# TensorE's idle products as tiles of 64 rows by 32 columns, eight side by side, in an attention and mixture-of-experts kernel

## The chip, the cores and the metric

The kernel runs on one core of a Trainium2 chip. The metric is the device time of one execution in microseconds; the profile shows one execution of the same program.

## The reference

A sequence of T = 4096 tokens of D = 256 numbers passes through one layer: attention with 16 heads, ALiBi bias and LoRA weights, a layer norm, a mixture of 8 experts of which each token takes 2, and a second layer norm.

```python
q, k, v = (lora(x, W, A, B) for each of q, k, v)        # x @ W.T + 2 * x @ B.T @ A.T
s = q @ k.T / 4 + slope[h] * (i - j), masked to j <= i
x = layernorm(x + softmax(s) @ v @ Wp.T)
gates, experts = top2(softmax(x @ Wg))                  # capacity CAP = 1076 slots for each expert
buf[expert * CAP + place] = x                           # what exceeds CAP is dropped
y = gelu(buf @ W1 + b1) @ W2 + b2
out = layernorm(x + sum of gate * y over the two experts of a token)
```

## The kernel before, in words

The program has two parts, each with an instruction stream per engine that is written out by hand. The first part projects block by block (8 blocks of 512 tokens), attends, and routes the tokens of blocks 0 to 6 between the attention's steps. The second part (`experts`) begins with the last block's routing (`Last`), then runs over the 8 experts, and ends with the layer norm.

TensorE has *idle products* at two places. They multiply data that happen to be there, write to a PSUM bank from which nobody reads them, and stand where the engine would otherwise wait.

*Lead-in.* `pe_warm(n, bank)` (lines 658 to 660) issues n bfloat16 products of the 128 x 128 corner of `sq` (all zero here) with its 512 columns, into `ps_r`. TensorE runs 13 of them, then the LoRA products for the keys (`pe_lora`, line 654, which contract only 8 rows), 3 more, the LoRA products for the queries, and then the first tiles of the projection (`pe_tile`, line 666). VectorE adds each LoRA result to the weights (`dve_weights`, line 761), and the first tile waits for that.

*Beside the scatters.* In `Last`, TensorE counts the tokens ahead of each token (`pe_count`, lines 1866 and 1867). From the counts VectorE makes the destinations, ScalarE and VectorE split the rows into two bfloat16 parts, and GpSimd scatters them to `slots_x` in 8 indirect DMAs (line 2030), each followed by an increment of `issued`; a memset (line 2212) gives the ninth. `Last.tensor` puts idle products between its waits for `issued`: 10 ahead of the first, 3 behind each of the first seven, 9 behind the eighth, 40 in all. Each is a float32 product of 128 x 128 with 256 columns.

Behind them TensorE transposes the first expert's rows (`transpose`, line 2394), which SyncE loads into `xe` (line 2330) once all scatters are complete. ScalarE copies them to `xs` (line 2464), and the expert's first products (`up`, line 2406) need those.

Every wait is on a semaphore, and every engine works in the order of its own stream. `ps_s` is the tile of six PSUM banks that the lead-in calls `banks(0)` to `banks(5)`; in the second part `ps_y` (two banks) and `ps_x` (two banks) are others.

Of the kernel before, what the change touches and what calls it, by code (L numbers as in the profile page):

```python
# [9 lines left out]
F32 = mybir.dt.float32  # L10
# [8 lines left out]
P = 128  # L19
# [6 lines left out]
QB = 512  # L26
NB = T // QB
KT = QB // P
# [25 lines left out]
HALF = 64  # L54
# [41 lines left out]
COLS = 4  # L96
# [391 lines left out]
class Project:  # L488
# [166 lines left out]
                           start=True, stop=True)  # L655
        mm.then_inc(j.lora_mm, 1)

    def pe_warm(j, pe, n, bank):
        for _ in range(n):
            pe.matmul(bank[:], j.sq[:, 0, 0:P], j.sq[:, 0, :], start=True, stop=True)  # L660

    def pe_tile(j, pe, n, k, out):
        m = TILE_ORDER[k]
# [588 lines left out]
def attend(nc, io, sb, psum, sem, dram, attnT, sums, flag, slots_x, r, out_stored):  # L1252
    with ExitStack() as st:
# [6 lines left out]
        ps_r = psum("ps_r", [P, QB], F32, st)  # L1260
# [9 lines left out]
        j = Project(io, lambda n, sh, dt: sb(n, sh, dt, st), sem, dram, flag, o, r,  # L1270
                    Space(r.x1[:, 2:].rearrange("p n t d -> p (n t d)")), Space(words))
        last = Space(o.mem[:, (o.mem.shape[1] - QB * (NP_ - FIRST_PAIR[NB - 1])):].bitcast(F32))
# [7 lines left out]
        with nc.Block() as block:  # L1280
            @block.sync
            def _(sp):
# [13 lines left out]
                for t in range(N_TURNS):  # L1296
# [35 lines left out]
                    if t in LOAD_AT:  # L1332
                        b = LOAD_AT[t]
                        for k in range(ACCS):
                            done = [job.stores for job in JOBS if job.number % ACCS == k and any(of == b for _, of, _ in job.heads)]
                            if done:
                                sp.wait_ge(out_stored[k], max(done))
                        r.load(sp, b, 0)
# [4 lines left out]
            def _(pe):  # L1343

                pe.wait_ge(j.hsel_set, 1)
                j.pe_warm(pe, 13, ps_r)
                j.pe_lora(pe, 1, banks)
                j.pe_warm(pe, 3, ps_r)
                j.pe_lora(pe, 0, banks)
                pe.wait_ge(j.weff_done, 2)  # L1350
                j.pe_tile(pe, 0, 0, banks(0))
# [696 lines left out]
class Last:  # L2048
# [24 lines left out]
    def tensor(l, pe, out, count, warm):  # L2073
        r, u = l.r, l.N % 2
        for c in (1, 0):
            for s in range(KT):
                if c == 0 or s == 0:
                    pe.wait_ge(r.scaled, l.BASE + (KT if c == 1 else KT + s + 1))
                mm = pe.matmul(out[:, s, 0:D + E], r.aT[:, u, c, s * P:(s + 1) * P], r.wp[:, c, :], start=(c == 1), stop=(c == 0))  # L2079
                if c == 0:  # L2080
                    mm.then_inc(r.y_mm, 1)
        r.pe_count(pe, l.N, count[:, 0:KT * E])


        for m in range(2 * KT + 1):
            if m >= 1:
                pe.wait_ge(l.issued, m)
            for _ in range(10 if m == 0 else 3 if m < 2 * KT else 9):
                pe.matmul(warm[:, 0:QB // 2], r.aT[:, u, 0, 0:P], r.aT[:, u, 0, 0:QB // 2], start=True, stop=True)  # L2089

    def stats(l, dve, s):
        r = l.r
# [169 lines left out]
def experts(nc, io, psum, slots_x, result, X, r, z, last):  # L2262
    sb, sem = X.sb, X.sem
    w1s, w2s, b1, b2, ident, ws, ye_mm = X.w1s, X.w2s, X.b1, X.b2, X.ident, X.ws, X.ye_mm
    with ExitStack() as st:
        warm = sb("warm5", [1, 1], F32)
# [11 lines left out]
        ps_h = psum("ps_h", [P, 4, QB], F32, st)  # L2278
        ps_y = psum("ps_y5", [P, 2, QB], F32, st)
        ps_x = psum("ps_x", [P, 2, 2 * QB], BF16, st)  # L2280
# [44 lines left out]
        with nc.Block() as block:  # L2325
            @block.sync
            def _(sp):
                def load(u, e):
                    z = SB[0][1]
                    sp.dma_start(xe[:, u, 0:z], xs_d[e, 0:z * P].rearrange("(k p) d -> p k d", p=P)).then_inc(x_first[u], 16)  # L2330
                    sp.dma_start(xe[:, u, z:ST - 1], xs_d[e, z * P:(ST - 1) * P].rearrange("(k p) d -> p k d", p=P)).then_inc(x_loaded[u], 16)
                    sp.dma_start(xe[0:LAST, u, ST - 1], xs_d[e, (ST - 1) * P:CAP]).then_inc(x_loaded[u], 16)

                last.sync(sp, X, io)
                load(0, 0)
                load(1, 1)
                with sp.Fori(0, E // 2 - 1) as i:
                    for u in range(2):
                        e = 2 * i + u
                        sp.wait_ge(ws, e * 2 + 2)  # L2340
                        sp.wait_ge(x_mm, e * ST + ST)
                        sp.wait_ge(entry_done, e * 4 + 4)
                        X.load_weights(sp, io, u, e + 2)
                        load(u, e + 2)
                for k in range(3):
                    sp.wait_ge(y_stored[k], 16 * (E * ST // 3))
                z.sync(sp)
# [30 lines left out]

            @block.tensor
            def _(pe):  # L2380
                last.tensor(pe, ps_h, ps_y[:, 0], ps_y[:, 1])
                pe.wait_ge(X.const, 16 * (E + 3))

                def transpose(e, i, u, k):
# [331 lines left out]
```

## Time and profile before

| | |
|---|---|
| time, median of 3 runs | 1236.36 us (1235.23 to 1239.9) |
| span of the profiled execution | 1237.8 us |
| TensorE busy | 1160.2 us, 94% |
| ScalarE busy | 904.4 us, 73% |
| VectorE busy | 634.1 us, 51% |
| GpSimd busy | 352.0 us, 28% |
| idle products beside the scatters, on the chain that ended last | 2% of the span |

The profiled execution has no time of its own beside its span of 1237.8 us; that is what its sums are made against. Of the page, the share of busy time says which engine is the fullest, and the chain that ended last says which of its work set the end. Starts are in microseconds from the first instruction. A matmul's duration holds the time in which its last results leave the array, which overlaps the next; the distance between starts is what a product costs in a stream. A float32 matmul is recorded as two, each of two passes over its columns.

### The profile page before, as it was taken

How to read it: one execution, taken by the hardware profiler on the slowest of the kernel's cores; microseconds unless marked ns; L12 is line 12 of the kernel's file. 1: busy time of each engine (PE TensorE's matmuls, PEld its weight loads, DVE VectorE, ACT ScalarE, POOL GpSimd, SP SyncE). 2: the span in 40 equal slices, each digit the busy share in tenths (PEclk: the TensorE clock that was granted, in tenths of full speed). 3: DMA queues.
4: the chain of work that ended last, by engine and by line, in shares of the span. 5: the costliest groups of instructions: out<-in, count | busy, mean ns of one | idle time of the engine just before them, and what ended most of it. 6: DMA issues, size and time to landing. Idle time of an engine off the chain costs nothing. (4 is left out here: it accounts for less than half of the span.)

```text
span 1237.8 us, 24554 instructions
## 1 busy us (share of the span) xinstructions
PE 1160.2 (94%) x8768; PEld 508.1 (41%) x8768; DVE 634.1 (51%) x1802; ACT 904.4 (73%) x1181; POOL 352.0 (28%) x391
## 2 busy tenths in 40 slices
PE   9999999999999999999999989699999999999980
PEld 4332222222222222222222111277677787787770
DVE  5644343232366335624353203548767768768746
ACT  3889999999999899999999989344435435435314
POOL 5421111111123112232122120024453552552440
PEclk9999999999999999999999989799999999999995
DMA  6843421322321331224120101533433523421226
GB/s 178 175 110 72 106 73 51 89 75 80 87 76 51 108 78 52 65 72 108 38 73 31 47 14 26 178 119 107 114 57 98 129 26 111 123 33 13 28 23 271
DMA packets 84098, 104.09 MB, mean 84 GB/s; under 512 B 15415, under 2 KB 69308, under 8 KB 83984
## 3 DMA queue, kind: packets, MB, share of 16 engines
q1 hardware_dynamic: 66520, 76.80, 21.9%
q0 software_dynamic: 15968, 24.12, 9.3%
q10 hardware_dynamic: 1496, 1.68, 0.4%
q8 instruction: 67, 1.10, 0.4%
q14 instruction: 47, 0.39, 0.1%
HBM read 56.88 MB, written 47.96 MB: 85 GB/s over the span
## 5 line engine op out<-in xcount | busy, mean ns | idle before, releaser
L1487 ACT ACTIVATE prob<-ps_s 128x1024 f32<-128x1024 f32 (+4 forms) x841 | 706.0, 995 | 47.9 <-PE ps_s L1376 46.3
L1393 PE MATMUL ps_o<-prob,v_aug 128*17 128x512 f32 (+3 forms) x3236 | 423.8, 570 | 3.5 <-DVE acc L1571 2.8
L1376 PE MATMUL ps_s<-qop,kop 51*128 51x512 f16 (+3 forms) x1618 | 261.1, 370 | 18.6 <-ACT prob L1487 6.6
L1376 PEld LDWEIGHTS ps_s<-qop,kop 51*128 51x128 f16 x1618 | 62.4, 93 | 387.3 <-ACT prob L1487 366.2
L2425 PE MATMUL ps_y<-w2s,hs 128*128 128x256 bf16 (+1 forms) x1728 | 189.1, 273 | 0.6 <-DVE yb L2511 0.6
L2406 PE MATMUL ps_h<-xs,w1s 128*128 128x384 bf16 (+1 forms) x1152 | 179.9, 315 | 5.1 <-ACT hid L2473 4.4
L2473 ACT ACTIVATE hid<-ps_h,b 128x384 f32<-128x384 f32 (+1 forms) x192 | 105.1, 560 | 108.5 <-PE ps_h L2406 83.6
L1571 DVE COPY acc<-ps_o 32x512 f32<-32x512 f32 (+2 forms) x108 | 74.2, 687 | 191.2 <-PE ps_o L1393 189.7
L2425 PEld LDWEIGHTS ps_y<-w2s,hs 128*128 128x128 bf16 (+1 forms) x1728 | 157.6, 99 | 17.6 <-DVE yb L2511 0.7
L2362 POOL DMA_INDIRECT result<-y,entry x72 | 111.8, 1553 | 175.4 <-DVE y L2516 140.6
L1523 POOL TENSOR_SCALAR_AFFINE_SELECT prob<-prob 128x256 f32<-128x256 f32 (+1 forms) x179 | 69.2, 397 | 311.3 <-ACT prob L1487 308.9
L2406 PEld LDWEIGHTS ps_h<-xs,w1s 128*128 128x128 bf16 x1152 | 111.2, 98 | 68.7 <-ACT hid L2473 7.1
L2030 POOL DMA_INDIRECT slots_x<-xsplit,dest_all x64 | 63.4, 990 | 253.2 <-ACT prob L1487 197.4
L2464 ACT ACTIVATE xs<-ps_x 128x512 bf16<-128x512 bf16 (+1 forms) x72 | 40.0, 570 | 105.0 <-PE ps_x L2394 104.9
L1393 PEld LDWEIGHTS ps_o<-prob,v_aug 128*17 128x17 f32 x3236 | 59.5, 95 | 136.8 <-issue 82.2
L2525 DVE CAST hs<-hid 128x384 bf16<-128x384 f32 (+1 forms) x192 | 91.9, 479 | 39.9 <-ACT hid L2473 39.4
L2527 DVE TENSOR_TENSOR hs<-hid,hs 128x384 bf16<-128x384 f32 (+1 forms) x192 | 102.1, 532 | 6.6
L2516 DVE TENSOR_SCALAR y<-yb,weight 128x256 f32<-128x256 f32 (+1 forms) x72 | 45.7, 635 | 13.5 <-DMA result<-y,entry 8.7
L825 DVE CAST x_all<-ps_r 128x256 f16<-128x256 f32 x24 | 10.2, 424 | 79.8 <-PE ps_r L676 79.8
L2511 DVE TENSOR_TENSOR yb<-ps_y,b 128x256 f32<-128x256 f32 x64 | 27.0, 422 | 43.2 <-PE ps_y L2425 42.9
L2259 POOL TENSOR_TENSOR w1s<-w,w1s 128x2048 bf16<-128x2048 f32 x7 | 28.5, 4073 | 45.5 <-ACT w1s L2253 26.3
L1897 DVE TENSOR_TENSOR slogit<-ps_r,xg 128x8 f32<-128x8 f32 x28 | 4.7, 166 | 71.0 <-PE ps_r L1861 70.9
(204 smaller groups left out, 788.3 us busy)
## 6 DMA issues: line engine op xcount, KB each, us to landing
w<-in_W SPq DMA_DIRECT2D x16, 1024.0 KB, 7.5
slots_x<-empty POOLq DMA_DIRECT2D x12, 520.0 KB, 4.1
qop<-fparts_q SPq DMA_DIRECT2D x42, 128.0 KB, 4.9
xe<-slots_x SPq DMA_DIRECT2D x8, 650.0 KB
aT<-attnT SPq DMA_DIRECT2D x16, 256.0 KB
x_all<-in_x SPq DMA_DIRECT2D x8, 512.0 KB
result<-x_all SPq DMA_DIRECT2D x8, 512.0 KB
x_all<-result SPq DMA_DIRECT2D x8, 512.0 KB, 6.6
```

The source lines that it names most:

```text
L1376: mm = pe.matmul(ps_s[:, u.p % SLOTS_S, e, a.q0:], o.key(e, a.h, a.kt), o.query(e, a.h, a.b, a.q0), start=True, stop=True)
L1393: mm = pe.matmul(ps_o[32 * c:32 * c + VW, a.q0:], o.v[:, a.kt, a.h], prob[:, t % RING, c % 2, c // 2, a.q0:], start=a.first, stop=a.last)
L1487: act.activation(prob[:, t % RING, n, e:z, q0:], ps_s[:, u.p % SLOTS_S, e:z, q0:], ACT.Exp, scale=1.0 / (SCALE * SCALE)).then_inc(exp_done, 1)
L1523: pool.affine_select(own, own, [[0, z - e], [1, P]], ALU.is_ge, 0.0, base=0, channel_multiplier=-1).then_inc(masked, 1)
L1571: dve.tensor_copy(acc[rows, a], ps_o[rows]).then_inc(evicted, 1)
L2030: pool.indirect_dma_start(out=r.slots_x, out_offset=bass.IndirectOffsetOnAxis(ap=r.dest_all[:, n, m:m + 1], axis=0), in_=r.xsplit[:, m // ...
L2362: pool.indirect_dma_start(out=result, out_offset=bass.IndirectOffsetOnAxis(ap=entry[0:n, u, k:k + 1], axis=0), in_=y[0:n, k % 3], in_offse ...
L2406: mm = pe.matmul(ps_h[:, q % 4, 0:w], w1s[:, u, i1, c, m * P:(m + 1) * P], xs[:, u, i2, c, a:a + w], start=(t == 0 and c == 0), stop=(t == ...
L2425: mm = pe.matmul(ps_y[to:to + n, (ST * u + k) % 2, 0:D], hs[:, (3 * u + sbk) % 2, i1, m, o:o + n], w2s[:, u, i2, m, :], start=(t == 0 and ...
L2473: act.activation(hid[:, q % 4, 0:w], ps_h[:, q % 4, 0:w], ACT.Gelu_apprx_tanh, bias=b1[:, e, q % HC:q % HC + 1]).then_inc(gelu, 1)
L2525: dve.tensor_copy(hs[:, sl, 0, q % HC, 0:w], hid[:, q % 4, 0:w]).then_inc(h_high, 1)
L2527: dve.tensor_tensor(hs[:, sl, 1, q % HC, 0:w], hid[:, q % 4, 0:w], hs[:, sl, 0, q % HC, 0:w], ALU.subtract).then_inc(h_low, 1)
```

## The change

Both kinds of idle product become groups of eight tiles: two halves of 64 rows by four quarters of 32 columns, each tile a matmul of its own, with the lower rows' results in one bank and the upper rows' in another. Each tile has its own weights of 64 x 32 and moves 512 columns.

In the lead-in there are 13 and 3 groups where there were 13 and 3 products, on the same bfloat16 zeros. Beside the scatters there is a `turn`: a group of eight in bfloat16 (the constant `before`, its 128 columns read four times over), a group in float32 (512 columns of `aT`), and again one in bfloat16. Three turns take the place of 10 products, one turn that of each 3, and three turns that of the last 9: 13 turns, or 312 matmuls, for 40.

```diff
--- before.py
+++ after.py
@@ -655,9 +655,13 @@
                            start=True, stop=True)
         mm.then_inc(j.lora_mm, 1)
 
-    def pe_warm(j, pe, n, bank):
+    def pe_warm(j, pe, n, banks):
         for _ in range(n):
-            pe.matmul(bank[:], j.sq[:, 0, 0:P], j.sq[:, 0, :], start=True, stop=True)
+            for c in range(COLS):
+                for e in range(2):
+                    rows = slice(HALF * e, HALF * e + HALF)
+                    pe.matmul(banks[e][32 * c:32 * c + 32, :], j.sq[rows, 0, 32 * c:32 * c + 32], j.sq[rows, 0, :],
+                              start=True, stop=True)
 
     def pe_tile(j, pe, n, k, out):
         m = TILE_ORDER[k]
@@ -1343,9 +1347,9 @@
             def _(pe):
 
                 pe.wait_ge(j.hsel_set, 1)
-                j.pe_warm(pe, 13, ps_r)
+                j.pe_warm(pe, 13, (ps_r, banks(0)))
                 j.pe_lora(pe, 1, banks)
-                j.pe_warm(pe, 3, ps_r)
+                j.pe_warm(pe, 3, (ps_r, banks(0)))
                 j.pe_lora(pe, 0, banks)
                 pe.wait_ge(j.weff_done, 2)
                 j.pe_tile(pe, 0, 0, banks(0))
@@ -2085,8 +2089,22 @@
         for m in range(2 * KT + 1):
             if m >= 1:
                 pe.wait_ge(l.issued, m)
-            for _ in range(10 if m == 0 else 3 if m < 2 * KT else 9):
-                pe.matmul(warm[:, 0:QB // 2], r.aT[:, u, 0, 0:P], r.aT[:, u, 0, 0:QB // 2], start=True, stop=True)
+            for _ in range(3 if m == 0 else 1 if m < 2 * KT else 3):
+                l.turn(pe, warm, r.aT[:, u, 0].rearrange("p (s t) -> p s t", s=KT), r.before[:].unsqueeze(1).broadcast_to([P, KT, P]))
+
+    def turn(l, pe, banks, full, half):
+
+        l.tiles(pe, banks, half)
+        l.tiles(pe, banks, full)
+        l.tiles(pe, banks, half)
+
+    def tiles(l, pe, banks, data):
+
+        for c in range(COLS):
+            for e in range(2):
+                rows = slice(HALF * e, HALF * e + HALF)
+                pe.matmul(banks[e][32 * c:32 * c + 32, :].rearrange("p (s t) -> p s t", s=KT), data[rows, 0, 32 * c:32 * c + 32], data[rows],
+                          start=True, stop=True)
 
     def stats(l, dve, s):
         r = l.r
@@ -2378,7 +2396,7 @@
 
             @block.tensor
             def _(pe):
-                last.tensor(pe, ps_h, ps_y[:, 0], ps_y[:, 1])
+                last.tensor(pe, ps_h, ps_y[:, 0], (ps_y[:, 1], ps_x[:, 0].bitcast(F32)))
                 pe.wait_ge(X.const, 16 * (E + 3))
 
                 def transpose(e, i, u, k):
```

TensorE's stream at the start of the program, before the change (`prob` holds the LoRA weights here, `sq` the zeros):

```order
L660 MATMUL ps_r<-sq 128x512 [waits hsel_set]
L660 MATMUL ps_r<-sq 128x512 x12
L654 MATMUL ps_s<-prob 128x256 [waits lora_k]
L654 MATMUL ps_s<-prob 128x256
L660 MATMUL ps_r<-sq 128x512 x3
L654 MATMUL ps_s<-prob 128x256 [waits lora_loaded]
L654 MATMUL ps_s<-prob 128x256
```

And with the change, from the last two tiles of the first 13 groups to the first two of the next three:

```order
L663 MATMUL ps_r<-sq 32x512
L663 MATMUL ps_s<-sq 32x512
L654 MATMUL ps_s<-prob 128x256 [waits lora_k]
L654 MATMUL ps_s<-prob 128x256
L663 MATMUL ps_r<-sq 32x512
L663 MATMUL ps_s<-sq 32x512
```

Each product with an output of 128 x 512 has become eight with 32 x 512, in turn into `ps_r` and `ps_s`; the waits stand where they stood.

TensorE's stream beside the last scatters, before, from the counts to the first transposes:

```order
L1866 MATMUL ps_y<-counts,before 128x32 [waits count_done]
L1867 MATMUL ps_y<-ahead,ones 128x32
L2089 MATMUL ps_y<-aT 128x256 x10
L2089 MATMUL ps_y<-aT 128x256 [waits last_issued]
...
L2089 MATMUL ps_y<-aT 128x256 [waits last_issued]
L2089 MATMUL ps_y<-aT 128x256 x8
L2394 MATMUL ps_x<-ident,xe 128x128 [waits x_out,e_const,xe_first0]
```

With the change, the border between the first bfloat16 group and the first float32 group; each group has eight such rows:

```order
L2106 MATMUL ps_y<-before 32x512
L2106 MATMUL ps_x<-before 32x512
L2106 MATMUL ps_y<-before 32x512
L2106 MATMUL ps_x<-before 32x512
L2106 MATMUL ps_y<-aT 32x512
L2106 MATMUL ps_x<-aT 32x512
```

The border shows the two kinds in turn. And the stage's end, the last bfloat16 tiles and the first transpose:

```order
L2106 MATMUL ps_y<-before 32x512
L2106 MATMUL ps_x<-before 32x512
L2106 MATMUL ps_y<-before 32x512
L2106 MATMUL ps_x<-before 32x512
L2412 MATMUL ps_x<-ident,xe 128x128 [waits x_out,e_const,xe_first0]
```

The transposes wait for the same as before, and write the tile that is now the second bank of the idle products.

## Rows read from the trace of the kernel before

**Rows 1.** The page: span, and the TensorE clock in 40 slices
```profile
span 1237.8 us, 24554 instructions
PE   9999999999999999999999989699999999999980
PEclk9999999999999999999999989799999999999995
```

**Rows 2.** Timeline and line 660, TensorE, lead-in (start us, us, engine line)
```profile
1.40 5.46 PE L660 MATMUL ps_r<-sq 128*128 128x512 bf16 x13 [1.40 <-POOL hsel L1499]
6.79 1.13 PE L654 MATMUL ps_s<-prob 8*128 8x256 f32 x4
7.85 0.82 PE L660 MATMUL ps_r<-sq 128*128 128x512 bf16 x3
9.65 8.83 PE L666 MATMUL ps_s<-x_all 128*128 128x512 f32 x16
...
L660 PE MATMUL ps_r<-sq x16: 379/634/634, 1.4 to 8.3; 128*128 128x512 bf16 x16
```

**Rows 3.** Busy time by stretches, lead-in; PEclk is the granted clock
```profile
1.40:3.40 2.00, 2.00 (x5) 0.73 (x6) 1.87 (x4) 1.04 (x1) 0.01 (x1) 1.00 0.60 181
6.86:9.65 2.79, 2.79 (x11) 1.46 (x11) 0.76 (x2) 0.43 (x1) 2.79 (x7) 1.00 0.91 204
12.00:13.00 1.00, 1.00 (x2) 0.34 (x1) 0.00 (x0) 0.00 (x0) 0.00 (x0) 0.50 0.00 0
```

**Rows 4.** Timeline of VectorE, lead-in
```profile
8.04 0.76 DVE L761 SCALAR_TENSOR_TENSOR x_all<-ps_s,prob 128x256 f32<-128x256 f32 x2 [4.00 <-PE ps_s L654]
9.83 0.75 DVE L761 SCALAR_TENSOR_TENSOR x_all<-ps_s,prob 128x256 f32<-128x256 f32 x2 [1.04 <-PE ps_s L654]
```

**Rows 5.** Timeline of TensorE beside and behind the last scatters
```profile
802.93 20.30 PE L2089 MATMUL ps_y<-aT 128*128 128x256 f32 x80
823.07 0.61 PE L2394 MATMUL ps_x<-ident,xe 128*128 128x128 bf16 x8
```

**Rows 6.** Busy time by stretches, beside the last scatters
```profile
807.00:808.00 1.00, 1.00 (x4) 0.82 (x3) 0.00 (x0) 0.93 (x2) 0.69 (x2) 0.50 0.99 338
808.00:810.00 2.00, 2.00 (x9) 1.68 (x9) 0.00 (x0) 0.00 (x0) 1.40 (x2) 0.85 0.45 146
```

**Rows 7.** Timeline of GpSimd and SyncE there; landing of xe
```profile
816.11 0.09 POOL L2212 MEMSET last_done<- 1x1 f32 x1
817.53 0.37 SPq L2330 DMA_DIRECT2D xe<-slots_x  x1
...
DMA to landing us min/median/max: 3.1/4.1/5.0
```

**Rows 8.** The chain that ended last, in order of time
```profile
803.09 20.14 PE ps_y L2089 x80
```

**Rows 9.** Timeline of TensorE, pairs and column tiles
```profile
34.72 0.60 PE L1376 MATMUL ps_s<-qop,kop 51*128 51x512 f16 x4
35.26 0.40 PE L686 MATMUL ps_r<-sq,hsel 128*32 128x512 bf16 x4
35.48 0.60 PE L1393 MATMUL ps_o<-prob,v_aug 128*17 128x256 f32 x8
```

**Rows 10.** Transposes of 52 rows: timeline, and groups by form
```profile
872.88 0.27 PE L2394 MATMUL ps_x<-ident,xe 52*128 52x52 bf16 x4
...
L2394 PE MATMUL ps_x<-ident,xe 52*128 52x52 bf16 x4 | 0.3, 184 | 0.0
```

**Rows 11.** Timeline, stretches and code packets around 734 us
```profile
734.02 1.03 PE L1376 MATMUL ps_s<-qop,kop 51*128 51x512 f16 x4 [3.38 <-issue]
...
736.90:740.20 3.30, 3.30 (x16) 0.34 (x16) 0.43 (x1) 1.94 (x2) 0.00 (x0) 0.50 0.00 0
740.40:743.00 2.60, 2.60 (x24) 0.39 (x22) 0.05 (x1) 2.60 (x3) 0.29 (x1) 1.00 0.06 13
...
q8 instruction: 67, 1.10, 0.4%
```

## The prediction

> **What bounds the kernel now.** I read three things: the page for the level of TensorE, the timeline of TensorE around the two places where the idle products stand, and the busy time by stretches for the clock there. The span is 1237.8 us, and TensorE is 9 tenths busy at 9 tenths of the clock nearly everywhere [rows 1]. The reader should see that neither place is idle time that can be lengthened for nothing.
>
> In the lead-in TensorE runs 13 products, the first LoRA products, 3 products, the second LoRA products and then the first tile, with no idle time between them [rows 2]. VectorE's first weights start at 8.04, after the LoRA products of 6.79 to 7.92, the second at 9.83, and the tile needs the first of them [rows 2, 4]. So a microsecond more in line 660 moves the projection by up to a microsecond. The clock is 1.00 in the stretch from 6.86 and falls to 0.50 behind it; the tile of 9.65 still runs at half clock between 12 and 13 [rows 2, 3]. (For the stretch 1.40 to 3.40 the record says 1.00, but 13 products of 512 columns took 5.46 us: (5.46 - 0.63)/12 = 0.40 each, near 512/1.2 GHz = 0.43. It was half clock; 0.63 is the longest of one, taken from the group's row.)
>
> Beside the last scatters TensorE is busy from 802.93 to 823.2 with 40 float32 products, 80 records since a float32 product is recorded as two [rows 5]. The clock is 0.50 until 808 and 0.85 from 808 to 810, so 0.6 of these 2 us were still at half and it rose at 808.6 [rows 6]. The 5.7 us at half and 14.4 us at full clock hold 80 records: 5.7/2w + 14.4/w = 80 gives w = 0.216 us, a product 0.43 at full and 0.86 at half clock. What do these products hold up? GpSimd's memset at 816.11, behind the eighth scatter, frees the last nine; the load of xe is issued at 817.53, the quickest landing in that stretch took 3.1 us, so it is there at about 820.7 [rows 7]. The transposes that need it start at 823.07, right behind the last idle product, and the expert's products need what they bring [rows 5]. So the idle products end some 2.3 us late, because 5.7 us of them ran at half clock, and their end is on the path that sets the end: the chain goes 20.14 us through line 2089 [rows 8].
>
> **The change, part by part.** *Lead-in.* 16 products of 128 rows by 128 columns and 512 columns moved become 16 groups of eight, 64 by 32, each moving 512. If the eight run together a group lasts what a product did. That they do rests on two rows: two halves of 51 rows by 128 columns in two banks run as pairs, four matmuls of 512 columns in 0.60 us, and four tiles of 128 by 32 with 512 columns last 0.40 together [rows 9]; one after the other, either four would need 4 x 0.216 and the last one's end, over 0.86. The trace never has both splits at once; I take the product of the two, 8 side by side. What remains is the skew of starting them: eight in the two tile rows cost under 0.01 us. Sum 0. The LoRA products between them use 8 rows, so the number of changes of shape is the same as before; 0 again.
>
> *Scatters.* A turn is 16 bfloat16 tiles (two groups of 512) and 8 float32 tiles (one group, 4 x 512 cycles): 6 x 512 cycles, 6 x 0.216 = 1.30 us at full clock, exactly three of the old products (3 x 2 x 0.216 = 1.30). So in the seven waits for `issued` 1 to 7, and in the last, where 9 become 3 turns, nothing changes. Ahead of the first wait 10 products (4.32 at full clock) become 3 turns (3.89): -0.43. All of it comes through, since the stream is late and never waits: 3 turns from 803 end at about 809.7 (5.6 us at half clock are 2.8 of the 3.9 needed, the rest 1.1 behind 808.6), long after the first scatter was issued.
>
> *Change of shape.* From 51-row pairs (34.72, two of 0.216, so streamed until 35.15) to the 128 by 32 tiles at 35.26 there are 0.11 us; from these to the next of their shape at 35.48 there are 0.22, the stream itself and nothing more [rows 9]. The stage gets two such changes, behind the counts and ahead of the transposes: +0.2. The sum is -0.43 + 0.2 = -0.2 us on the last stage and 0 on the lead-in.
>
> *Issue.* The new code has 8 matmuls and 8 weight loads in 0.216 us. The nearest row is the transposes of 52 rows: four in 0.27 us with a mean of 0.184, so (0.27 - 0.18)/3 = 0.029 us for a matmul with its load [rows 10]. Eight are 0.23, 0.02 over the stream: with 26 bfloat16 groups beside the scatters at most +0.5; below, nothing. A float32 group has 16 records for 0.86 us and is never bound by this, and in the lead-in a group has 0.43. As the float32 group lets the queue fill again I take 0, and +0.5 is an end of the range. Against this stands the Trainium skill, page "TensorE: Matmul & The Clock Gate", section "Wait — 56ns, not 53.3ns?": a sequencer without its hardware decoder spends about 62 ns on each matmul, and that binds once the array's own work is shorter. By that figure the sum, as an estimate, would be some 10 us higher. The trace disagrees with its 0.029 us a matmul.
>
> The profiled execution has a span of 1237.8 us, and its sum is 1237.8 - 0.2 = 1237.6; the span lies 1.4 us over the median of the runs shown, 1236.36, from which the same step gives 1236.1. The kernel's own runs spread from 1235.23 to 1239.9, so that anything within 0.5% (6.2 us) is about what a measurement can't tell from no change.
>
> **The rivals.** *The clock doesn't rise on tiles (slower).* Streams of 64-row tiles alone may not bring it up. For it: the record shows TensorE without a gap from 6.86 to 9.65, much of it products of 8 rows, and a fall behind them [rows 2, 3]; what the products are seems to matter. Against it: from 736.9 to 740.2, at half clock, TensorE did nothing but 51-row pairs and column tiles, and the clock was 1.00 right behind them; the whole attention, made of the same, holds 9 tenths [rows 1, 11]. But most of that time are column tiles of 128 rows, so tiles of 64 alone are not tried. The price: 13 turns at half clock are 13 x 2.59 = 33.7 us, ending at 802.93 + 33.7 + 0.3 = 836.9 where it was 823.1, +13.8. In the lead-in the 3 products go from 0.82 to about 1.4 (+0.6) and the LoRA behind it loses 0.5; the first expert products start at half clock, like the tile from 9.65 to about 13, whose 3.4 us there hold 1.7 of work, so another 1.7. Together +16.6: 1253. It decides when the clock is still 0.5 at 821, that is when 12.4 us more than before are run at half.
>
> *The two halves run one after the other (slower).* Then a turn is 2.59 us at full clock; the stage needs 33.7 of full-clock work, 2.8 of it done by 808.6, and ends at 839.5, +16.4; the lead-in adds 13 x 0.43 + 3 x 0.22 = 6.2. 1259. Against it the pairs [rows 9].
>
> *Issue is the bound (slower).* The 0.029 us may be the pace of a queue filled beforehand; a steady stream may come at twice that. Then a bfloat16 group needs 8 x 0.058 = 0.46 where it had 0.22: in some 25 groups at full clock (22 beside the scatters, 3 in the lead-in) +6.1. In 11 float32 groups 16 records need 0.93 for 0.86, +0.8; in 17 bfloat16 groups at half clock 0.46 for 0.43, +0.5. Together +7.4: 1243.5. For it: nowhere does this trace keep up such a pace for more than four matmuls; against it: those four [rows 10], and the quads of [rows 9]. It decides from about 0.054 us a matmul.
>
> *Code comes late (slower or the same).* The change adds some 420 program rows to TensorE, and code comes in packets (67 packets, 1.10 MB, 16 KB each) [rows 11]. The worst wait on "issue" of TensorE that I found is 3.38 us, ahead of 734.02, at a branch [rows 11]. Straight code shows none. One such stall: 1239.5; three, one in the lead-in where the DMA engines are full and two at the scatters: 1246.
>
> *The clock rises earlier (faster, but not by 0.5%).* Should eight tiles bring it up sooner than one product does, the stage could be at full clock from its start: the stream would end at about 820.2, held by the memset of 816.11 plus three turns, and the load's landing at 820.7 takes over: -2.3 at most. The tile of 9.65 at full clock would give another 1.7. 1232.1.
>
> **How the numbers follow.** No change but the small one (same clock, eight together): 0.72. Clock stays low: 0.09. Halves one after the other: 0.03. Issue-bound: 0.04. Code late: 0.06, most of it one stall. Clock earlier: 0.06. The predicted time is the first: 1236.1. Its own range, with the spread of the kernel's own runs, the 0.5 of issue and the 0.4 of changes of shape, is 1234 to 1240. The range goes down to 1231.5 (clock earlier) and up to 1243 (one or two code stalls); what is left out are the slow cases beyond it, 0.15. Slower by over 0.5%, above 1242.5: clock low 0.09, halves 0.03, half of the issue case 0.02, more than one code stall 0.01, together 0.15. Faster by over 0.5% needs more than both clock gains together: 0.02. Same: 0.83.
>
> **What would show it.** Right: the products of the lead-in take 5.4 to 5.6 us and those behind them 0.8; the turns' 13 x 24 tiles run from 803 for 19.5 to 20.5 us, gap-free, with 8 starts inside 0.05 us; the clock rises at about 808.6; transposes start about 20.1 us behind the counts. Wrong: the clock at 0.5 beyond 812; tiles of the lower half that start when those of the upper end; a busy share of TensorE under 9 tenths in the turns with "issue" as what ended the idle time; or a clock that rises earlier and transposes that then wait for xe. What would make the prediction wrong is above all the first, since the trace has no stretch with tiles of 64 rows alone.

## The result and the profile after

The changed kernel takes 1249.35 us (1247.53 to 1252.13, 4 runs) against 1237.0 us (1235.23 to 1239.9, 4 runs) of the kernel before on the same chip: a ratio of 1.01, 95% interval 1.0079 to 1.012. It is slower by about 12 us where no change was forecast (1236.1, up to 1243). The profiled execution is its run of 1247.53 us. Its page, span and TensorE's rows of the 40 slices and of the code queue (packets, MB, share), answers to [rows 1] and [rows 11]:

```profile
span 1245.5 us, 25450 instructions
PE   9999999999999999999999989599999999999980
PEclk9999999999999999999999999799999999999995
q8 instruction: 80, 1.31, 0.5%
```

The clock's row looks no worse. One slice of TensorE has fallen from 6 to 5, and 80 packets of code came instead of 67.

The lead-in is as forecast. TensorE's timeline there, to be held against [rows 2] and, for the group at full clock, [rows 9]:

```profile
1.40 0.60 PE L663 MATMUL ps_r<-sq 64*32 64x512 bf16 x1 [1.40 <-POOL hsel L1503]
...
1.42 0.61 PE L663 MATMUL ps_s<-sq 64*32 64x512 bf16 x1
1.80 0.63 PE L663 MATMUL ps_r<-sq 64*32 64x512 bf16 x1
...
6.03 1.13 PE L654 MATMUL ps_s<-prob 8*128 8x256 f32 x4
7.09 0.39 PE L663 MATMUL ps_r<-sq 64*32 64x512 bf16 x1
...
7.32 0.38 PE L663 MATMUL ps_r<-sq 64*32 64x512 bf16 x1
...
7.53 0.38 PE L663 MATMUL ps_r<-sq 64*32 64x512 bf16 x1
```

Eight tiles of a group start within some 0.02 us, and at full clock groups follow each other at 7.09, 7.32 and 7.53, so 0.21 to 0.23 us for eight matmuls with eight loads. The first tile of the projection starts at 8.92 (9.65 before).

Beside the scatters it is another picture. Busy time by stretches of the changed kernel (PE busy (x), PEld, DVE, ACT, POOL, PEclk, DMA share, GB/s); [rows 5, 6] are those of before, where the same stretches are all full. The number behind each x counts the records that touch a stretch, so one that crosses a border stands in both rows, and a float32 matmul is two records:

```profile
804.00:806.00 2.00, 2.00 (x41) 0.58 (x26) 0.00 (x0) 0.49 (x2) 1.70 (x2) 1.00 0.73 242
806.00:808.00 2.00, 1.36 (x10) 0.27 (x7) 0.00 (x0) 0.00 (x0) 1.39 (x3) 1.00 0.09 29
808.00:810.00 2.00, 0.66 (x9) 0.35 (x8) 0.00 (x0) 0.00 (x0) 1.70 (x2) 1.00 0.18 62
810.00:812.00 2.00, 1.22 (x8) 0.21 (x5) 0.00 (x0) 0.00 (x0) 1.39 (x3) 0.61 0.13 45
812.00:814.00 2.00, 2.00 (x9) 0.20 (x4) 1.07 (x1) 0.00 (x0) 0.75 (x2) 0.53 0.16 55
814.00:816.00 2.00, 2.00 (x55) 1.47 (x61) 2.00 (x2) 0.00 (x0) 0.00 (x0) 1.00 0.42 87
```

The clock is 1.00 from 804, so the tiles do bring it up. Then from 806 to 814 TensorE starts 25 records in 8 us, where 53 start in the two microseconds behind. TensorE's timeline shows the pattern, and GpSimd's what stands beside it:

```profile
806.91 0.37 PE L2106 MATMUL ps_x<-before 64*32 64x512 bf16 x1 [0.32 <-issue]
806.93 0.38 PE L2106 MATMUL ps_y<-before 64*32 64x512 bf16 x1
806.94 0.38 PE L2106 MATMUL ps_x<-before 64*32 64x512 bf16 x1
807.64 0.37 PE L2106 MATMUL ps_y<-before 64*32 64x512 bf16 x1 [0.32 <-issue]
808.36 0.37 PE L2106 MATMUL ps_x<-before 64*32 64x512 bf16 x1 [0.35 <-issue]
...
809.77 0.37 PE L2106 MATMUL ps_y<-before 64*32 64x512 bf16 x1 [1.00 <-issue]
```

```profile
802.70 0.99 POOL L2034 DMA_INDIRECT slots_x<-xsplit,dest_all  x1 [51.17 <-DVE xsplit L2199]
...
811.71 0.98 POOL L2034 DMA_INDIRECT slots_x<-xsplit,dest_all  x1 [0.30 <-issue]
812.66 0.09 POOL L2230 MEMSET last_done<- 1x1 f32 x1
```

A few matmuls start together and the next ones come 0.7 or 1.4 us later, and the idle time ends by "issue": nothing in the program is waited for. Each tile still lasts 0.37 to 0.38 us, as at full clock in the lead-in, so what is late is its start. It happens while GpSimd's eight scatters run: their DMA packets last from 805.1 to 813.7. No packet of TensorE's code comes between 801.0 and 816.8, so the stream picks up at 814 without one. Behind the pauses the clock falls again (0.61 and 0.53 in the rows from 810 to 814). I call this the starved stretch.

A second loss lies 200 us later, at the jump back to the experts' loop. TensorE's timeline of the changed kernel, and then of the kernel before, at the same place:

```profile
1018.49 1.50 PE L2443 MATMUL ps_y<-w2s,hs 128*52 128x256 bf16 x24
1022.51 1.78 PE L2424 MATMUL ps_h<-xs,w1s 128*128 128x384 bf16 x5 [2.52 <-issue]
```

```profile
1014.64 1.50 PE L2425 MATMUL ps_y<-w2s,hs 128*52 128x256 bf16 x24
1016.07 3.10 PE L2406 MATMUL ps_h<-xs,w1s 128*128 128x384 bf16 x18
```

The branch itself took 3.32 us (0.24 before), and behind it the clock is at half for 3.4 us. No packet of code came between 1005.9 and 1111.1 before, so I read that the second pass of the loop ran from code that was still loaded; now one comes every 4 to 18 us all through the pass.

**The sum.** From the two profiled executions: counts 3.4 us earlier (799.46 for 802.90), counts to the first `up` product 29.75 us for 22.45 (+7.3), from there to TensorE's last product 380.47 for 376.47 (+4.0), the rest -0.1: 7.7, the difference of the spans. The 3.4 are no gain: four kernels below (g4_end, h5_both, i1_direct, i3_add) are the kernel before up to 1190 us, and their counts start at 800.76, 803.50, 800.88 and 797.63. Without them it is 7.3 + 4.0 = 11.3, near the 12.35 between the medians; the last microsecond stays open.

### The profile page after: what moved, and what is told of

Its sections match the earlier page's. It is cut to its first block, busy times and chain, and to the rows that moved or that the text cites. A ratio compares the mean times of both kernels' runs of the same rounds, so it can differ in the third digit from the quotient of the medians.

```text
span 1245.5 us, 25450 instructions
## 1 busy us (share of the span) xinstructions
PE 1162.1 (93%) x9216; PEld 501.6 (40%) x9216; DVE 634.7 (51%) x1802; ACT 904.2 (73%) x1181; POOL 351.0 (28%) x391
## 3 DMA queue, kind: packets, MB, share of 16 engines
q8 instruction: 80, 1.31, 0.5%
## 4 chain that ended last, share of the span: by engine, by line
PE 70%; ACT 16%; DVE 7%; issue 5%; DMA 1%; ACTq 0%; POOL 0%; SPq 0%; POOLq 0%; DVEq 0%
PE ps_o L1397 21%; ACT prob L1491 15%; PE ps_y L2443 14%; PE ps_h L2424 12%; PE ps_s L1380 12%; PE ps_r L696 3%; PE ps_r L1865 2%; PE ps_r L680 2%; PE ps_x L2412 1%; DVE hs L2543 1%; PE ps_y L2106 1%; PE ps_x L2106 1%; ACT x_all L2632 1%; DVE statsc L2670 1%; DVE y L2534 0%
```

## The experiments

Every run was profiled. "Stage" is from the last counts to the first `up` product, "loop" from there to TensorE's last product, "gap" TensorE's idle time at the loop's jump; times are medians, ratios with their 95% interval, each made with runs of the kernel before on that kernel's own chip (medians 1236.39 to 1238.19 there). Stage, gap and loop are from one profiled execution each.

| kernel | stage | gap | loop | time | ratio to before |
|---|---|---|---|---|---|
| before | 22.45 | 0 | 376.47 | 1237.0 | |
| after | 29.75 | 2.5 | 380.47 | 1249.35 | 1.01 (1.0079 to 1.012) |
| e1_lead | 22.57 | 0 | 377.30 | 1237.32 | 0.9995 (0.9979 to 1.0012) |
| e2_scatter | 30.36 | 2.8 | 380.97 | 1250.08 | 1.0093 (1.0058 to 1.0128) |
| e3_small | 29.81 | 0 | 377.29 | 1246.84 | 1.006 (1.004 to 1.0081) |
| e4_f32 | 29.87 | 0 | 377.30 | 1243.08 | 1.0041 (1.0025 to 1.0056) |
| g1_pad64 | 31.93 | 2.7 and 2.6 | 385.44 | 1253.93 | 1.0133 (1.0108 to 1.0158) |
| g2_before_pad | 22.32 | 2.6 | 381.67 | 1242.6 | 1.004 (1.0025 to 1.0056) |
| g3_nowait | 30.22 | 2.5 | 380.66 | 1249.56 | 1.0109 (1.008 to 1.0137) |
| h2_pad128 | 31.38 | 0 | 376.47 | 1245.81 | 1.0071 (1.0056 to 1.0087) |
| h3_fewer | 20.19 | 0 | 376.52 | 1236.14 | 0.9992 (0.9978 to 1.0006) |
| i2_fewer_lead | 20.13 | 2.5 and 2.6 | 383.95 | 1242.54 | 1.0042 (1.0027 to 1.0056) |
| j1_fewer_lead_pad | 20.05 | 0 | 377.53 | 1237.96 | 1.0003 (0.999 to 1.0015) |

### Are the tiles at fault?

*e1_lead* is the kernel before with the new `pe_warm` alone, *e2_scatter* the changed kernel with the old `pe_warm`.

> Only the 16 lead-in products are groups of eight tiles; the products beside the scatters are those of before. Theory A (TensorE's code comes too late where many short matmuls stand behind each other, and where the loop over the experts no longer stays loaded): the lead-in itself costs nothing, the stream beside the scatters lasts about 20 us as before, and the time is that of before, unless the 224 more instructions alone bring the loop's stall at its branch, which would be +4 us. Theory B (tiles as such are slow or don't hold the clock): the lead-in products take over 6 us and the time rises by 1 to 3 us.

> Only the products beside the scatters are tiles; the lead-in is that of before. Theory A: a stretch of some 9 us with two or three matmuls per 0.7 us stands again in the stream beside the scatters, which lasts 26 to 28 us for 20; the time is 7 to 12 us over before. Theory B: the stream is slow too, but evenly, without such a stretch.

The lead-in's tiles cost nothing, and the turns hold all of the loss. *e3_small* has no tiles, but nearly as many matmuls as the turns; *e4_f32* has the same tiles in float32 alone, which need half the pace.

```diff
-            for _ in range(10 if m == 0 else 3 if m < 2 * KT else 9):
-                pe.matmul(warm[:, 0:QB // 2], r.aT[:, u, 0, 0:P], r.aT[:, u, 0, 0:QB // 2], start=True, stop=True)
+            for _ in range(24 * (3 if m == 0 else 1 if m < 2 * KT else 3)):             # e3_small
+                pe.matmul(warm[:, 0:P], r.before[:], r.before[:], start=True, stop=True)
+            for _ in range(5 if m == 0 else 1 + m % 2 if m < 2 * KT else 4):            # e4_f32
+                l.tiles(pe, warm, r.aT[:, u, 0].rearrange("p (s t) -> p s t", s=KT))
```

> No tiles: beside the scatters the 40 float32 products are 312 bfloat16 products of 128x128 with 128 columns, as many matmuls as the tiles, behind the same waits, and 24 of them fill the same 1.3 us. Their result is used by nobody, as before. Theory A (number and pace of instructions): the same stretch of starved TensorE as with the tiles, 26 to 28 us for 20, and +7 to +12 us. Theory B (tiles): the stream lasts 20 to 21 us and the time is that of before.

> Tiles of 64x32, but float32 alone: 20 groups of eight in place of 13 turns, 160 matmuls for 312, the same array time, half the pace. The lead-in is that of before. Theory A: a much shorter starved stretch or none, the stream at 20 to 23 us, 0 to +4 us. Theory B: as slow as with the turns, +7 us.

Both are starved in the same place. Stretches of e3_small, and behind them one of e4_f32:

```profile
808.00:810.00 2.00, 1.25 (x17) 0.79 (x14) 0.00 (x0) 0.00 (x0) 1.63 (x2) 1.00 0.18 60
810.00:812.00 2.00, 0.50 (x3) 0.17 (x3) 0.00 (x0) 0.00 (x0) 1.46 (x2) 1.00 0.18 61
```

```profile
812.00:814.00 2.00, 1.88 (x7) 0.24 (x5) 0.00 (x0) 0.00 (x0) 1.39 (x3) 1.00 0.08 26
```

So it is neither the shape nor the alternation. In the profiled execution the half pace of e4_f32 did not help as expected: its stage is 7.4 us longer. That execution took 1247.96 us, though, the longest of nine, and the median of 1243.08 is 4.9 us over that of its own runs of before, less than the 8.2 that stage and loop have in the profile (e3_small has 8.65 for the same 8.2). So how much the half pace saves in the other executions stays open. Neither kernel has the gap at the loop: the two losses are separate.

### The starved stretch: waits, place in the program, or the scatters?

*g3_nowait* takes TensorE's waits for `issued` away (nothing reads what the idle products write). *g4_end* is the kernel before with the 13 turns added at the end of TensorE's stream, where no such scatter runs.

```diff
-            if m >= 1:
-                pe.wait_ge(l.issued, m)                      # g3_nowait, in the changed kernel
...
                 over_experts(pe, one)
+                pe.wait_ge(y_sum, E * ST + 2)                # g4_end, in the kernel before
+                for _ in range(13):
+                    last.turn(pe, ...)
```

> The changed kernel without TensorE's waits on the scatters as issued: the 13 turns come back to back, about 17 us of products. Theory C (while GpSimd issues and writes its scatters, TensorE's instructions come slowly): still starved, about 4 instructions in 0.7 us between 805 and 814 us, so that the stretch from counts to transposes is 25 us or more and the time stays within 2 us of the changed kernel. Theory D (the waits break up the supply of instructions): dense turns of 1.3 us from first to last, products done some 17 to 18 us after the counts, the transposes then by the landing of xe at about 20 us, and a time of 1241 to 1243.

> The kernel before with the 13 turns of tiles put at the end of TensorE's program instead, behind the last products of the experts and the wait for y's sums, where no scatter runs. Theory C (beside the scatters only): turns of about 1.3 us at full clock (2.6 us at half) without gaps of more than 0.3 us, 17 to 20 us in all at full clock, and the time of the kernel before, 1237 to 1239, as nothing waits for them or they end before the output does. Theory A (312 small matmuls in straight code are starved wherever they stand): gaps of 0.6 to 0.8 us after every 4 instructions, 25 us or more for the 13 turns.

The waits are not it (stage 30.22). At the end of the program the same turns are dense, their first tile starting at 1202.08 and their last at 1218.9, 16.8 us, with the time as before (1239.35, ratio 1.0011, 0.9996 to 1.0026), though the DMA engines are full there. Stretches of g4_end:

```profile
1204.00:1206.00 2.00, 2.00 (x58) 1.06 (x50) 0.00 (x0) 0.00 (x0) 0.83 (x1) 1.00 0.03 0
1210.00:1212.00 2.00, 2.00 (x65) 1.34 (x52) 1.21 (x4) 0.00 (x0) 0.00 (x0) 1.00 1.02 399
```

Two more runs move the scatters and leave the turns. *h1_hold* is g3_nowait with the last turn's matmul incrementing `issued` and GpSimd waiting for that ahead of its first scatter. *h5_both* is g4_end with eight such scatters more, to the same rows, beside the turns at the end.

```diff
+                pool.wait_ge(l.issued, 1)                    # h1_hold, ahead of the first scatter
...
                 over_experts(pool, one)
+                for m in range(2 * KT):                      # h5_both, GpSimd
+                    pool.wait_ge(r.scattered, NB * KT * 2 * 16)
+                    alone(pool)
+                    r.scatter_rows(pool, last.N, m, r.scattered)
```

> The changed kernel with the 13 turns back to back behind the counts and GpSimd's eight scatters held back until the last turn has ended. Theory C (only beside these scatters do TensorE's instructions come slowly): all 13 turns are dense, 2.6 us each until the clock rises and 1.3 us then, 20 to 22 us in all with no idle time over 0.3 us at full clock, and 55 to 65 products started in every 2 us from the clock's rise on. The scatters, and with them the transposes, then come some 17 us later than in the changed kernel's own program of before, so a time of about 1253 to 1260. Theory A (the position in the program or the number of instructions starves it): the same stretch of 4 products per 0.7 to 1.4 us, 5 us behind the counts for 8 to 9 us, as in the changed kernel, with no scatter beside it.

> The kernel of the turns at the end of the program (dense there, 16.8 us) with eight scatters more of the same kind, issued by GpSimd behind its last one, beside those turns. Theory C: the dense stream is starved from about 1 us behind the first transfer of these scatters until their last, 4 products per 0.7 to 1.4 us for 8 to 9 us, so the 13 turns take 24 to 26 us. Theory A: the turns stay dense, 16.8 us.

Stretches of h1_hold, and its first scatter in GpSimd's timeline:

```profile
806.00:808.00 2.00, 2.00 (x64) 0.84 (x56) 0.00 (x0) 0.00 (x0) 0.00 (x0) 1.00 0.00 0
812.00:814.00 2.00, 2.00 (x64) 0.80 (x56) 0.00 (x0) 0.00 (x0) 0.00 (x0) 1.00 0.04 8
```

```profile
820.55 0.99 POOL L2034 DMA_INDIRECT slots_x<-xsplit,dest_all  x1 [69.13 <-POOLq L2230]
```

The same code at the same place is dense once no scatter runs: 13 turns in 18.9 us, the first 5 us at half clock. (The one execution took 1258.93 us, as the scatters come later.) And stretches of h5_both, whose scatters are issued from 1207.09 to 1216.19:

```profile
1206.00:1208.00 2.00, 2.00 (x59) 1.09 (x47) 0.00 (x0) 0.00 (x0) 1.68 (x2) 1.00 0.04 4
1208.00:1210.00 2.00, 2.00 (x31) 0.47 (x15) 0.00 (x0) 0.00 (x0) 1.39 (x3) 1.00 0.47 64
1210.00:1212.00 2.00, 1.83 (x14) 0.37 (x13) 0.00 (x0) 0.00 (x0) 1.70 (x2) 1.00 0.72 261
1212.00:1214.00 2.00, 0.78 (x4) 0.13 (x4) 1.19 (x4) 0.00 (x0) 1.39 (x3) 1.00 1.01 394
1214.00:1216.00 2.00, 0.65 (x6) 0.31 (x5) 1.83 (x8) 0.00 (x0) 1.58 (x2) 0.79 1.00 403
```

The dense turns become starved ones, 27.5 us for 16.8, longer than the 24 to 26 expected, the clock falling with them. Taken away and added, the scatters decide. h5_both, i1_direct and i3_add were run once each (1241.62, 1241.17 and 1236.62 us), and are read for their turns alone.

But not every scatter does this. The same plain ones run 56 times beside the attention, 2.4 us apart and more, each with packets for some 0.5 us. Beside 55 of them TensorE is never idle by "issue", though its matmuls start there at about 8 in a microsecond; at the last one lies the branch of [rows 11]. Beside the experts' scatters it never starves either. These accumulate into memory. *i1_direct* and *i3_add* are h5_both with another transfer each:

```diff
-                    r.scatter_rows(pool, last.N, m, r.scattered)
+                    pool.dma_start(r.slots_x[m * P:(m + 1) * P], r.xsplit[:, m // 2]).then_inc(r.scattered, 16)   # i1_direct
+                    pool.indirect_dma_start(..., compute_op=ALU.add).then_inc(r.scattered, 16)                    # i3_add
```

> The kernel with the turns and eight more transfers at the end, but the eight are direct ones of the same 128 rows each to fixed rows, from GpSimd's queue. If the indirect addresses matter, the 13 turns stay dense, about 17 us; if any transfer from GpSimd's queue starves TensorE, 24 to 26 us as with the scatters (there the 13 turns took about 24 us).

> The same kernel with the eight scatters accumulating in memory, as the experts' do, to the same rows (so these rows hold other values at the end). If the kind of write matters, the turns stay dense beside them, about 17 us, as beside the last two scatters of the experts; if only their number in a row or the rate of the products matters, they are starved as with the plain scatters, 4 products per 0.7 to 1.4 us.

One stretch of i1_direct and the eight transfers in GpSimd's timeline, then the same of i3_add, with one scatter of its eight:

```profile
1206.00:1208.00 2.00, 2.00 (x64) 0.96 (x56) 0.00 (x0) 0.00 (x0) 2.00 (x5) 1.00 0.90 160
```

```profile
1203.28 4.91 POOL L2395 DMA_DIRECT2D slots_x<-xsplit  x8
```

```profile
1206.00:1208.00 2.00, 2.00 (x66) 0.84 (x52) 0.01 (x1) 0.00 (x0) 1.70 (x2) 1.00 1.04 355
```

```profile
1207.40 1.56 POOL L2395 DMA_INDIRECT slots_x<-xsplit,dest_all  x1 [0.30 <-issue]
```

Both are dense, 17.2 and 16.6 us for the 13 turns (the 24 us that the expectation of i1_direct gives for h5_both are 27.5 in its trace). It takes the plain indirect scatters in close order: the same eight with `add` do nothing to TensorE, nor do direct transfers of the same blocks of rows from the same queue. The `add` takes GpSimd 1.56 us instead of 0.98, so these scatters start 1.86 us apart where the plain ones start 1.29 apart; whether the kind of write or this pace decides between the two, no run shows.

### The gap at the loop: number or place of the code?

Instructions that never run, put into the branch of a flag ahead of all this code, move what lies behind them. *g1_pad64* and *h2_pad128* are the changed kernel with 64 and 128 of them, *g2_before_pad* the kernel before with 170.

```diff
         with pe.If(flag):
             y.enter(pe)
+            for _ in range(64):          # 128, 170
+                pe.drain()
```

> The changed kernel with 64 instructions that never run added on TensorE, in the branch that a flag would take, so that all code behind them lies 64 instructions later. Theory of the loop's code (the jump back to the experts' loop at 1022 us has to wait for its code in the changed kernel because the last stretch of code fetched ahead of it had come too recently, which is a matter of where the code lies): the branch record falls from 3.3 us to some 0.3 us, the gap of 2.5 us there and the fall of the clock behind it are gone, counts of the queue of instruction packets fall from 80 to about 68, the stretch from the first up product to the last falls from 380.5 us to about 377, and the time is 3 to 4 us below the changed kernel: about 1245.5. The starved stretch beside the scatters stays (27.5 us from the counts to the transposes). Rival (the number of instructions fetched before the loop, not their place, sets it): the stall stays at 2.5 to 3.5 us and the time at 1249 or above.

> The kernel before with 170 instructions that never run added in the same branch, products untouched. Theory of the loop's code by place: the kernel before gets the stall at the loop's branch by itself, some 2.5 to 3.5 us, with the clock's fall behind it; from the first up product to the last 380 us instead of 376.5, and a time of 1241 to 1242. The stretch from the counts to the transposes stays at 20.2 us. Rival (only the added products can bring it): no stall, 1237 to 1238.5.

> The changed kernel with 128 instructions that never run ahead of the loop on TensorE; with 64 the last stretch of code ahead of the loop's jump came 6.6 us before it and the stall was there, without it 3.6 us. Theory of the loop's code by place: with 128 that distance is 9 to 10 us as in the kernel before; the branch takes 0.24 us, no gap stands behind it, the queue of instruction packets counts about 70, from the first up product to the last it takes 377 us, and the time is 1245 to 1247, 3 to 4 us under the changed kernel. Rival (with more instructions ahead of the loop it stalls wherever they lie): the stall of 2.5 us stays.

g1_pad64 missed: the gap stayed, and a second came behind it. The last packet of code ahead of the branch came 6.65 us before it, and the distance at which I expected no gap I had set from four kernels. g2_before_pad shows the point by itself: 170 instructions that never run bring the gap to the kernel before, and h2_pad128 takes it from the changed kernel. Timelines of g2_before_pad and h2_pad128:

```profile
1019.25 0.98 PE L2408 MATMUL ps_h<-xs,w1s 128*128 128x384 bf16 x5 [2.60 <-issue]
```

```profile
1020.83 1.50 PE L2445 MATMUL ps_y<-w2s,hs 128*52 128x256 bf16 x24
1022.26 1.96 PE L2426 MATMUL ps_h<-xs,w1s 128*128 128x384 bf16 x11
```

In h2_pad128 71 packets come instead of 80. Its time is 3.5 us under that of the changed kernel, though its stage is 1.6 us longer (31.38): behind the fall in the starved stretch the clock is at half for 6.8 us, where the changed kernel has 3.4. g1_pad64 has the same 6.8, and a stage of 31.93.

Over all profiled kernels, those whose last packet came 7.8 to 9.6 us ahead of the branch have no gap, those with 3.7 to 6.1 have one, and at 6.6 and 6.7 both occur. Packets come some 13 us apart here. What sorts them without a rest is the shift of the loop: the records of TensorE ahead of its branch beyond those of before, with the instructions added that never run. Only its remainder by 256 counts:

| shift | kernels | remainder | last packet ahead of the branch | gap |
|---|---|---|---|---|
| 0, 256, 1024 | before, g4_end, h5_both, i1_direct, i3_add; j1_fewer_lead_pad; h2_pad128 | 0 | 9.0 to 9.6 us | none |
| -32, 224, 480 | h3_fewer; e1_lead; e4_f32 | 224 | 7.8 to 8.1 | none |
| 464 | e3_small | 208 | 6.6 | none |
| 192, 960 | i2_fewer_lead; g1_pad64 | 192 | 6.7 | yes |
| 170 | g2_before_pad | 170 | 6.1 | yes |
| 672 | e2_scatter | 160 | 5.6 | yes |
| 896 | after, g3_nowait, h1_hold | 128 | 3.7 to 3.9 | yes |

So it is the place of the loop in its 16 KB blocks, not what was added. The Trainium skill, page "Runtime: NRT & Kernel Launch", section "Instruction fetch mechanics", says that TensorE's instruction memory takes 128 KiB, filled in order in blocks of 16 KiB (256 instructions), and that a taken branch to code outside a window of two blocks stalls for a fetch. The traces agree with the blocks (1.31 MB in 80 packets, and the remainders by 256). They don't agree with the two blocks: in the kernel before a whole pass of the loop, 94 us and 1697 records of TensorE or 6.6 times 256, needs no packet. The page also says that crossing a block is mostly hidden, and so it is in straight code here.

### A version that beats both?

If the stream of idle products ends late, fewer of them should help. *h3_fewer* is the kernel before with 1 product in place of the last 9, *i2_fewer_lead* that with the lead-in's tiles, *j1_fewer_lead_pad* the latter with 64 instructions of padding.

```diff
-            for _ in range(10 if m == 0 else 3 if m < 2 * KT else 9):
+            for _ in range(10 if m == 0 else 3 if m < 2 * KT else 1):
```

> The kernel before with 1 idle product behind the last scatter instead of 9, no tiles. If the stream of idle products is what the transposes wait for, and the first transposes' rows land before it ends: the stream from the counts to the transposes falls by 8 times 0.25 = 2.0 us to 18.2 us, and the time by up to 2 us: 1235.5 to 1237. If the rows land later than that, or the clock falls in the wait, the gain is under 0.5 us or turns into a loss.

> The kernel before with the tiles in the lead-in alone and 1 idle product behind the last scatter instead of 9. The stream from the counts to the transposes falls from 20.2 to about 18 us as it did with the 1 product alone; the lead-in's tiles change nothing or give the clock's rise a little earlier: 1234.5 to 1236.5, ratio to the kernel before 0.998 to 0.9995. If the two stand on luck of the clock alone, 1236 to 1238.

> The lead-in's tiles, 1 last product instead of 9, and 64 instructions on TensorE that never run. The last stretch of code before the loop's jump moves from 6.7 us to some 10 us ahead of it, so by the theory of place the branch takes 0.24 us again and both gaps behind it are gone; from the first up product to the last about 377 us instead of 384, and the time is 1235 to 1236.5, 0.05 to 0.2% under the kernel before. Rival (these edits cost the time themselves): 1240 or more.

All three stages are 2.3 to 2.4 us shorter. In h3_fewer the transposes start 17.9 us behind the counts, after 1.21 us without work; that the prediction puts the landing of xe 17.8 us behind them speaks for a wait for xe. i2_fewer_lead lost 7 us at the jump, which its expectation had not, and the padding took that back, though j1_fewer_lead_pad is still 1.5 us over what was expected of it. But no time is under that of before by more than its interval (0.9992 and 1.0003). None of them beats the kernel before; where the 2.3 us of the stage go in the medians stays open.

## Why the prediction was wrong

*What bounds the kernel*: right. The stream beside the scatters is on the path, 7.3 us more of it came through whole, and it did end 2.3 us late (h3_fewer, stage 20.19 for 22.45).

*Lead-in, 0*: right (e1_lead, 0.9995). Eight tiles run side by side as the product of two splits in [rows 9].

*The clock*: it rises on tiles alone; that rival (0.09) and the one of halves one after the other (0.03) fell. It came up 4.2 us behind the counts where 5.7 was forecast, and 4.9 behind them in h1_hold, with the same turns; g4_end, with the old products there, has 5.5.

*Scatters, -0.43 "since the stream is late and never waits", with issue at 0*: this is the step that failed. I counted waits on semaphores and the array's time and took the supply of instructions as given. Measured: 27.5 us from the counts to the transposes where about 20.1 was written, so +7.3 in the stage for -0.2. The turn itself was right, 1.29 us at full clock in g4_end (16.8 / 13).

*Issue, 0 to +0.5*: right about the pace that TensorE can keep (eight with their loads in 0.21 to 0.23 us, 0.027 us each), so the rival of 0.058 a matmul fell as a pace of the whole stream. The 62 ns that the Trainium skill, page "TensorE: Matmul & The Clock Gate", section "Wait — 56ns, not 53.3ns?", gives for a matmul with the hardware decoder off are not what the dense stretches show. It was wrong to carry a pace seen in one place to another: in the starved stretch a record took 8 us / 25 = 0.32 us. The large products of before run full through the same stretch [rows 6].

*Code comes late, 0.06*: the right kind of rival, wrongly sized and wrongly placed. "Straight code shows none" held, and one stall at a branch was worth about what I gave it: 2.5 us and a fallen clock behind it, 4.0 together. But the stall came from where the loop lies, which all code ahead of it decides. The change adds 384 matmuls, not the "some 420 program rows" that I took, and they are 896 instructions on the page of the profile (25450 for 24554), which leave a remainder of 128 by 256. I had read no row at that jump, where the trace of before shows that a whole pass of 94 us needs no packet, while six came in the 94 us ahead of it. By the page cited above TensorE holds 128 / 16 = 8 blocks, which I use as an estimate. A loop of 6.6 blocks touches seven or eight of them by its place, and is then one that a shift can push out; that it happens at this border is not shown.

The signs by which it could be told wrong did hold: a busy share under 9 tenths in the turns, with "issue" as what ended the idle time.

## What to carry to other kernels

Work in idle time is free only if its instructions are: count matmuls, not only the array's microseconds, above all beside plain indirect scatters that GpSimd issues close behind each other, and use there few and large products. When a change adds instructions ahead of a loop, look at the loop's branch and at the count of code packets before judging the change itself, and try a padding that makes the loop's shift against the old kernel a multiple of 256; otherwise 4 to 7 us of placement are put down to the edit. Idle time that ended by "issue" was a matter of supply here, and taking the waits away (g3_nowait) did not mend it.

## What the runs showed of the hardware

- While eight plain indirect scatters 1.29 us apart run (9 us), a stream of small matmuls shows 3 to 17 records in a row of 2 us; beside accumulating scatters to the same rows, direct transfers from the same queue, or output at 399 GB/s it shows 58 to 66. Single plain scatters beside the attention stop nothing. That it is the supply of instructions is read from "issue" and from the pattern. It is no fixed cap: the large products of before ran 9 [rows 6] to 11 records in such 2 us without a gap, where e3_small got 3, so a stream that uses its instructions slowly seems to stay ahead and one that has run dry does not catch up. That is argued, not shown, and which path the scatters share with TensorE's code no run shows.
- Eight tiles of 64 by 32 run fully side by side, 0.21 to 0.23 us for 8 x 512 columns with their loads, and the granted clock goes to its upper level on them (at 803.6 in the changed kernel, at 804.6 in h1_hold, behind tiles alone).
- 64 to 170 instructions that never run move the time by 3.5 to 5 us in either direction, and whether the loop's branch takes 0.24 us or over 3.3 goes by the loop's shift in records, by its remainder by 256: 0, 208 and 224 have no gap (11 kernels), 128 to 192 have one (7 kernels).
